# The near tables of a unit written in one transfer and read in one on another queue

## The chip, the cores and the metric

The kernel runs on one core of a Trainium2 chip. The core has TensorE (PE, matmuls), VectorE (DVE), ScalarE (ACT), GpSimd (POOL) and SyncE (SP, which only issues transfers), each with an instruction stream of its own, ordered against the others by semaphores. Transfers run on 16 DMA engines that all issuers share. The metric is the device time of one execution in microseconds.

## The reference

A block of DeBERTa-like attention is followed by a mixture of eight experts, each behind a layernorm. There are 4 x 1024 tokens of 256 channels, in 16 heads of 16. The part that matters here:

```python
scores = jnp.einsum('bhqd,bhkd->bhqk', q, k) / scale
rel = build_relative_position(S, S, BUCKETS, MAX_REL)
c2p_att = jnp.einsum('bhqd,hpd->bhqp', q, pos_k)
c2p = jnp.take_along_axis(c2p_att, clip(rel + ATT_SPAN, 0, 127), axis=-1)
p2c_att = jnp.einsum('bhkd,hpd->bhkp', k, pos_k)
p2c = jnp.swapaxes(jnp.take_along_axis(p2c_att, clip(-rel + ATT_SPAN, 0, 127), axis=-1), -1, -2)
scores = scores + (c2p + p2c) / scale
probs = jax.nn.softmax(scores, axis=-1)
ctx = jnp.einsum('bhqk,bhkd->bhqd', probs, v)
```

The positional terms depend on the distance of query and key alone, and from a distance of 128 on they are constant. So only a band of 384 keys around each block of 128 queries needs a table, the "near" tables; what is constant goes in through extra rows of the matmul ("far").

## The kernel before

The kernel has four stages in a row: `project` (projections of queries, keys and values), `attend` (attention), `mix` (output projection, layernorms, routing) and `experts`. The change touches only `attend`.

`attend` goes over 64 units (4 batches by 16 heads, `N`). A unit has 8 steps (`QT`), one for each block of 128 queries. Each engine runs one loop over s, from -20 (`AHEAD`) to 512 + 13 (`LAG`), and in each pass does some work for several steps at once, at fixed distances:

- `make_table(s + 20)`: PE makes the near values of a block, for both tables (content to position and position to content), and ScalarE's `keep_table` copies them to `table` in SBUF (lines 831 and 832).
- `score(s)`: PE adds the scores of a block; the near part (line 712) needs `near`.
- DVE's `look` and `level` find the row maxima and write the band without them.
- `flip(s - 13)`: PE turns the scores so that keys lie on partitions; ScalarE's `exponent` (line 839) writes the probabilities. `flip` of a step waits for the exponent of the step before it (one for each half).
- `weigh(s - 14)`: PE multiplies by the values (line 749).

Once per unit more is done: `turn_top` on PE at the end of the pass with s % 8 == 1 (line 757), which turns the row maxima for ScalarE's `keep_top` (lines 851 and 853); it waits for the splits that Pool makes of them (lines 926 to 936) and for the table copy of the same pass. The passes of a unit are called steps 0 to 7 here, by s % 8.

**The way of the near tables.** A near table must be skewed: partition p has to see its row shifted by p. The kernel does this through DRAM. `skew_write` stores `table` to `skew_d` with a row pitch of PITCH, and `skew_read` reads it back with a pitch of PITCH - 1. Both are issued by SyncE, and each unit has two halves, `h`. A half of the write is 1 MB in rows of 4 KB (line 629). A read is two transfers (line 639), of 384 KB each for the first half (spots 0 to 2) and of 640 KB each for the second (spots 3 to 7), in pieces of 1 KB. The read waits for the landing of its write (line 636). Then Pool corrects the edges in `near` in five operations for each half (lines 900, 903, 908, 913, 916), in passes that `steps` lists, and reports the half by `near_made`.

SyncE's order in a pass u over units: first half of the write of unit u+2, second half of the read of unit u+1, the four loads of queries and keys of unit u+4 (line 604, which from unit 6 on wait until `flip` is done with unit u-2), every second time three small loads of the far rows (line 615), then the second half of the write and the first half of the read of unit u+2, and the store of the context of unit u-2 (line 645). Each load of line 604 moves 96 KB and comes from a view whose outermost dimension is 3.

ScalarE's queue of its own carries, up to now, the turned maxima (line 853) and 18 small transfers at the start of the stage (line 866), which put constant rows beside the six buffers of queries and keys.

Of the kernel before, what the change touches and what calls it, by code (L numbers as in the profile page):

```python
# [152 lines left out]
def view(t, offset, dims):  # L153

    return bass.AP(tensor=t, offset=offset, ap=dims)
# [362 lines left out]
def attend(nc, sem, spent, masks, rows, split_d, far_d, v_d, skew_d, ctx_d):  # L518
# [14 lines left out]
    PIECES = ((0, 3), (3, QT))  # L533
# [5 lines left out]
    with ExitStack() as ctx:  # L539
# [11 lines left out]
        table = [sb(f"table{i}", [P, 2, 2, 4, SPOT]) for i in range(2)]  # L551
# [17 lines left out]
        rows_set = [sem(f"t_rows_set{i}") for i in range(BUFS)]  # L569
# [4 lines left out]
        skew_out = [[sem(f"t_skew_out{i}{h}") for h in range(2)] for i in range(2)]  # L574
        skew_in = [[sem(f"t_skew_in{i}{h}") for h in range(2)] for i in range(2)]
# [18 lines left out]
        def _(sp):  # L594
# [29 lines left out]
            def skew_write(n, h):  # L624
                sp.wait_ge(table_kept, n * QT + 4 * h + 4)
                if n >= 2:
                    sp.wait_ge(skew_in[n % 2][0], 16 * 2 * (n // 2))
                    sp.wait_ge(skew_in[n % 2][1], 16 * 2 * (n // 2))
                sp.dma_start(view(skew_d, n % 2 * (P * PITCH) + h * 4 * SPOT + 1, [[PITCH, P], [TABLE, 2], [1, 4 * SPOT]]),
                             table[n % 2][:, h, :, :, :].rearrange("p a u v -> p a (u v)")).then_inc(skew_out[n % 2][h], 16)  # L630

            def skew_read(n, h):
                if n >= 2:
                    sp.wait_ge(scored, (n - 2) * QT + 4 * h + 4)
                    sp.wait_ge(seen, (n - 2) * QT + 4 * h + 4)
                sp.wait_ge(skew_out[n % 2][h], 16 * (n // 2 + 1))
                lo, hi = PIECES[h]
                for tab in range(2):
                    sp.dma_start(near[n % 2][:, tab, lo:hi, P:W3],
                                 view(skew_d, n % 2 * (P * PITCH) + tab * TABLE + lo * SPOT + P,  # L640
                                      [[PITCH - 1, P], [SPOT, hi - lo], [1, SPOT]])).then_inc(skew_in[n % 2][h], 16)
# [6 lines left out]
            for u in range(-4, N + 3):  # L648
                if 0 <= u + 2 < N:
                    skew_write(u + 2, 0)  # L650
                if 0 <= u + 1 < N:
                    skew_read(u + 1, 1)
# [11 lines left out]
                if 0 <= u - 2 < N:  # L664
                    store(u - 2)
# [6 lines left out]
        def _(pe):  # L672
# [16 lines left out]
            def score(s):  # L689
# [6 lines left out]
                if t == 0 and n < BUFS:  # L696
                    pe.wait_ge(rows_set[n], 16 * 3)
# [123 lines left out]
        def _(act):  # L821
            def keep_table(x):
                n, u = x // QT, x % QT
                h = u // 4
                act.wait_ge(table_made, x + 1)
                if u % 4 == 0 and n >= 2:
                    act.wait_ge(skew_out[n % 2][h], 16 * (n // 2))
                    act.wait_ge(side_kept, (n - 2) * 2 + h + 1)
                wide = table[n % 2][:, h, :, u % 4, :]
# [16 lines left out]

            def keep_top(n):
# [15 lines left out]
            for i in range(BUFS):  # L863
                for dst, src in ((quest[i][KROWS:FAR, :], ones[0:3, :]), (after[i][FAR:ROWS, :], after_rows[:, :]),
                                 (before[i][FAR:ROWS, :], before_rows[:, :])):
                    nc.scalar.dma_start(dst, src).then_inc(rows_set[i], 16)
            for s in range(-AHEAD, TS + LAG + 1):
# [7 lines left out]
                if s % QT == 4 and 0 <= s // QT + 1 < N:  # L875
                    twin(s // QT + 1)
# [769 lines left out]
```

## Time and profile before

| | |
|---|---|
| median of 3 runs | 1870.73 us (1870.19 to 1876.40) |
| the profiled execution | 1863.67 us, its span 1861.8 us |
| PE busy | 1708.2 us (92%) |
| DVE busy | 1417.6 us (76%) |
| ACT busy | 1163.0 us (62%) |
| POOL busy | 1057.3 us (57%) |
| SyncE's queue in the DMA engines | 393.28 MB, 64.7% of the 16 engines' span |
| ScalarE's queue in the DMA engines | 21.10 MB, 3.6% |
| mean DMA rate | 229 GB/s |

`attend` begins at about 134 us and ends at about 1330 us, and so has two thirds of the span. The page's second part, 40 slices of 46.5 us, shows PE at nine tenths or more from the fifth slice to the 29th with a granted clock of ten tenths. The three slices at the start of the stage and the slices behind it are less full. Durations in the rows are those of instructions; for a transfer the profile has the time of its issue, and as "to landing" the time from the issue to the semaphore. "Idle before, releaser" is what ended an engine's wait. In the waits of SyncE's queue the waiting line is named first, and the operation that released it last.

### The profile page before, as it was taken

What the parts mean: (1) busy time and instruction counts of PE and PEld (TensorE: products, weight loads), DVE (VectorE), ACT (ScalarE), POOL (GpSimd) and SP (SyncE); (2) the same over time, 40 slices, a digit from 0 to 9 for tenths busy, and PEclk for the clock granted to TensorE, in tenths of its full rate; (3) what the DMA queues carried; (4) which work ended last, traced back from release to release, by engine and by line L of the source; (5) the groups of instructions that cost most, each with busy time, mean ns of one, the idle gap of its engine ahead of it and who ended that gap; (6) DMA issues with size and microseconds to landing.
All of it is one profiled execution on the core that took longest, in us unless ns stands there. A gap on an engine that the chain in (4) does not pass through costs nothing. (4 is left out here: it accounts for less than half of the span.)

```text
span 1861.8 us, 41287 instructions
## 1 busy us (share of the span) xinstructions
PE 1708.2 (92%) x13752; PEld 1164.0 (63%) x13752; DVE 1417.6 (76%) x4111; ACT 1163.0 (62%) x2784; POOL 1057.3 (57%) x1260
## 2 busy tenths in 40 slices
PE   7953899999999999999999999999869967999997
PEld 4531565666666666666666666666435656999996
DVE  4751898999999999999999999999534453555553
ACT  6843577788887888888888888787613441222221
POOL 0002777777777777877778777788214321333332
PEclk9985899999999999999999999999955566999998
DMA  5976787878778887788887877877065424666662
GB/s 152 302 259 214 250 277 261 278 256 284 263 257 296 267 276 262 268 285 267 278 276 253 288 260 264 274 262 244 19 169 182 139 74 137 208 189 201 201 198 68
DMA packets 297313, 426.33 MB, mean 229 GB/s; under 512 B 35773, under 2 KB 238545, under 8 KB 297008
## 3 DMA queue, kind: packets, MB, share of 16 engines
q1 hardware_dynamic: 285764, 393.28, 64.7%
q10 hardware_dynamic: 7596, 21.10, 3.6%
q0 software_dynamic: 3744, 9.31, 1.4%
q8 instruction: 112, 1.84, 0.4%
q14 instruction: 97, 0.79, 0.1%
HBM read 245.85 MB, written 178.05 MB: 228 GB/s over the span
## 5 line engine op out<-in xcount | busy, mean ns | idle before, releaser
L839 ACT ACTIVATE t_probsT<-t_flip 128x512 f32<-128x512 f32 x1024 | 626.0, 614 | 201.8 <-PE t_flip L735 148.0
L785 DVE TENSOR_REDUCE t_most<-t_scores 128x1 f32<-128x640 f32 (+1 forms) x512 | 435.0, 850 | 82.1 <-PE t_scores L712 78.8
L804 DVE TENSOR_SCALAR t_band<-t_band,t_top 128x384 f32<-128x384 f32 (+1 forms) x512 | 413.9, 809 | 0.0
L749 PE MATMUL t_sum_ps<-t_probsT,t_vals 128*32 128x256 f32 x4096 | 327.7, 392 | 0.2 <-ACT t_probsT L839 0.2
L831 ACT COPY t_table<-t_table_ps 128x388 f32<-128x388 f32 x512 | 247.9, 484 | 56.3 <-issue 29.0
L916 POOL TENSOR_TENSOR t_near<-t_near,masks 128x768 f32<-128x768 f32 (+1 forms) x128 | 273.5, 2137 | 0.0
L789 DVE CUSTOM_DVE_ANT_0 t_band<-t_scores,t_near 128x384 f32<-128x384 f32 (+1 forms) x512 | 261.6, 511 | 0.0
L735 PE MATMUL t_flip<-masks,t_band 128*128 128x128 f32 x1408 | 261.1, 274 | 0.0
L712 PE MATMUL t_scores<-masks,t_near 128*128 128x128 f32 x1408 | 241.8, 275 | 5.0 <-POOLq L919 5.0
L705 PE MATMUL t_scores<-t_afters,t_quests 105*128 105x256 bf16 (+3 forms) x1024 | 244.0, 288 | 1.3 <-DVE t_most L789 1.3
L900 POOL TENSOR_TENSOR t_near<-t_near,masks 128x384 f32<-128x384 f32 (+1 forms) x128 | 147.1, 1149 | 124.1 <-DMA t_near<-skew_d 117.5
L712 PEld LDWEIGHTS t_scores<-masks,t_near 128*128 128x128 f32 x1408 | 181.7, 143 | 44.5 <-POOLq L919 6.9
L705 PE MATMUL t_scores<-t_befores,t_quests 105*128 105x256 bf16 (+3 forms) x768 | 193.5, 292 | 0.0
L684 PE MATMUL t_table_ps<-rows,t_quests 96*128 96x194 bf16 x512 | 129.7, 253 | 57.5 <-DMA t_quests<-split_d 24.5
L735 PEld LDWEIGHTS t_flip<-masks,t_band 128*128 128x128 f32 x1408 | 163.6, 142 | 0.7
L728 PE MATMUL t_flip<-t_quests,t_befores 108*128 108x512 bf16 (+3 forms) x512 | 161.0, 316 | 0.8 <-ACT t_probsT L839 0.7
L728 PE MATMUL t_flip<-t_quests,t_afters 108*128 108x512 bf16 (+3 forms) x512 | 158.3, 309 | 0.5 <-ACT t_probsT L839 0.2
L1612 PEld LDWEIGHTS e_hid_ps<-e_xT,e_w 128*128 128x128 f32 x1248 | 148.1, 195 | 5.7 <-ACT e_xT L1478 3.7
L1612 PE MATMUL e_hid_ps<-e_xT,e_w 128*128 128x128 f32 x1248 | 148.6, 278 | 3.1 <-ACT e_xT L1478 3.1
L913 POOL TENSOR_TENSOR t_near<-t_near,masks 128x384 f32<-128x384 f32 (+1 forms) x128 | 147.9, 1155 | 0.0
L728 PEld LDWEIGHTS t_flip<-t_quests,t_befores 108*128 108x128 bf16 x512 | 48.9, 96 | 157.0 <-issue 102.3
L832 ACT COPY t_table<-t_table_ps 128x124 f32<-128x124 f32 x512 | 144.3, 282 | 0.0
(194 smaller groups left out, 2670.2 us busy)
## 6 DMA issues: line engine op xcount, KB each, us to landing
skew_d<-t_table SPq DMA_DIRECT2D x128, 1024.0 KB, 9.3
t_near<-skew_d SPq DMA_DIRECT2D x128, 640.0 KB, 8.1
t_near<-skew_d SPq DMA_DIRECT2D x128, 384.0 KB, 7.3
e_w<-in_L_ffn_W_dram ACTq DMA_DIRECT2D x39, 512.0 KB
e_w<-in_L_ffn_W_dram SPq DMA_DIRECT2D x39, 512.0 KB
split_d<-p_part SPq DMA_DIRECT2D x32, 384.0 KB, 3.3
t_afters<-split_d SPq DMA_DIRECT2D x128, 96.0 KB
t_quests<-split_d SPq DMA_DIRECT2D x128, 96.0 KB
```

What stands on the lines that cost most here:

```text
L705: nc.tensor.matmul(out[:, at:at + size], quest[i][0:XROWS, t * P:(t + 1) * P], keys[0:XROWS, piece[0] * P:piece[0] * P + size], start=at % ...
L712: last = nc.tensor.matmul(out[:, (j - lo) * P:(j - lo + 1) * P], near[n % 2][:, 1, j, (t - j + 1) * P:(t - j + 2) * P], ident, start=False ...
L728: last = nc.tensor.matmul(out[:, (a - lo) * P:(z - lo) * P], keys[:, j * P:(j + 1) * P], quest[i][:, a * P:z * P], start=first, stop=False ...
L735: last = nc.tensor.matmul(out[:, (t - lo) * P:(t - lo + 1) * P], band[n % 2][:, t, at:at + P], ident, start=False, stop=True, is_transpose ...
L749: last = nc.tensor.matmul(sum_ps[32 * g:32 * g + 32, 0:2 * P], vals[b % 2][:, j, h * VDIM:h * VDIM + 32], probsT[s % 3][:, g * 2 * P:(g + ...
L785: nc.vector.tensor_reduce(most[:, c, 1:2], out[:, wide:S], AX.X, ALU.max)
L789: nc.vector.tensor_tensor_reduce(band[n % 2][:, t, 0:wide], out[:, 0:wide], near[n % 2][:, 0, t, at:at + wide], 1.0, -3.0e38, ALU.add, ALU ...
L804: nc.vector.tensor_scalar(band[n % 2][:, t, 0:wide], band[n % 2][:, t, 0:wide], top[n % 2][:, t:t + 1], None, ALU.subtract).then_inc(level ...
L831: nc.scalar.copy(ends, table_ps[:, :, 0:FEW].rearrange("p a (e v) -> p a e v", e=2))
L839: nc.scalar.activation(probsT[s % 3][:, half * 512:(half + 1) * 512], flip_ps[half][:, :], ACT.Exp, scale=SCALE).then_inc(expd, 1)
L916: nc.gpsimd.tensor_tensor(tail, tail, masks[:, 1, :].unsqueeze(1).unsqueeze(1).to_broadcast([P, 2, many, P]), ALU.mult).then_inc(edge_made, 1)
L1612: last = nc.tensor.matmul(hid_ps[s % 2][:, c, :], w1[s % WB][:, f, c * P:(c + 1) * P], xT[s % 2][:, f, :], start=(f == 0), stop=(f == 1))
```

## The change

The halves go. `table` gets the layout [P, 2, QT, SPOT], so that a unit's tables lie in one piece of 16 KB per partition. `skew_write(n)` is one transfer of 2 MB by SyncE, issued when all eight blocks of the unit are kept. `skew_read(n)` is one transfer of 2 MB, issued by ScalarE on its own queue in the pass s = 8(n-1), behind the second exponent of that pass; from unit 2 on it waits until unit n-2 is scored and seen, and always for the landing of the write. SyncE's order is now: loads, far loads, write, store. The values of the first batch and the clearing of the old semaphores come later. Pool's steps are set anew: the first half begins two passes later, and its first two operations wait for the whole read. The 18 transfers of constant rows become three, with a source that repeats six times.

The diff, cut to its core:

```diff
-    PIECES = ((0, 3), (3, QT))
-        table = [sb(f"table{i}", [P, 2, 2, 4, SPOT]) for i in range(2)]
+        table = [sb(f"table{i}", [P, 2, QT, SPOT]) for i in range(2)]
-            def skew_write(n, h):
-                sp.wait_ge(table_kept, n * QT + 4 * h + 4)
+            def skew_write(n):
+                sp.wait_ge(table_kept, n * QT + QT)
                 if n >= 2:
-                    sp.wait_ge(skew_in[n % 2][0], 16 * 2 * (n // 2))
-                    sp.wait_ge(skew_in[n % 2][1], 16 * 2 * (n // 2))
-                sp.dma_start(view(skew_d, n % 2 * (P * PITCH) + h * 4 * SPOT + 1, [[PITCH, P], [TABLE, 2], [1, 4 * SPOT]]),
-                             table[n % 2][:, h, :, :, :].rearrange("p a u v -> p a (u v)")).then_inc(skew_out[n % 2][h], 16)
-
-            def skew_read(n, h):
-                if n >= 2:
-                    sp.wait_ge(scored, (n - 2) * QT + 4 * h + 4)
-                    sp.wait_ge(seen, (n - 2) * QT + 4 * h + 4)
-                sp.wait_ge(skew_out[n % 2][h], 16 * (n // 2 + 1))
-                lo, hi = PIECES[h]
-                for tab in range(2):
-                    sp.dma_start(near[n % 2][:, tab, lo:hi, P:W3],
...
+                    sp.wait_ge(skew_in[n % 2], 16 * (n // 2))
+                sp.dma_start(view(skew_d, n % 2 * (P * PITCH) + 1, [[PITCH, P], [1, PITCH]]),
+                             table[n % 2][:, :, :, :].rearrange("p a u v -> p (a u v)")).then_inc(skew_out[n % 2], 16)
...
             for u in range(-4, N + 3):
-                if 0 <= u + 2 < N:
-                    skew_write(u + 2, 0)
-                if 0 <= u + 1 < N:
-                    skew_read(u + 1, 1)
                 if 0 <= u + 4 < N:
                     load_unit(u + 4)
                 if 0 <= u + 2 < N and u % FARS == 0:
                     load_far(u + 2)
-                if u == -4:
+                if 0 <= u + 2 < N:
+                    skew_write(u + 2)
+                if 0 <= u - 2 < N:
+                    store(u - 2)
+                if u == -1:
                     load_vals(0)
+                if u == 1:
                     for semaphore in spent:
                         sp.sem_clear(semaphore)
-                if 0 <= u + 2 < N:
-                    skew_write(u + 2, 1)
-                    skew_read(u + 2, 0)
...
+            def skew_read(n):
+                if n >= 2:
+                    act.wait_ge(scored, (n - 1) * QT)
+                    act.wait_ge(seen, (n - 1) * QT)
+                act.wait_ge(skew_out[n % 2], 16 * (n // 2 + 1))
+                nc.scalar.dma_start(near[n % 2][:, :, :, P:W3].rearrange("p a u v -> p (a u) v"),
+                             view(skew_d, n % 2 * (P * PITCH) + P, [[PITCH - 1, P], [SPOT, 2 * QT], [1, SPOT]])
+                             ).then_inc(skew_in[n % 2], 16)
...
-            for i in range(BUFS):
-                for dst, src in ((quest[i][KROWS:FAR, :], ones[0:3, :]), (after[i][FAR:ROWS, :], after_rows[:, :]),
-                                 (before[i][FAR:ROWS, :], before_rows[:, :])):
-                    nc.scalar.dma_start(dst, src).then_inc(rows_set[i], 16)
+            for dst, src in ((quests[KROWS:FAR, :, :], ones[0:3, :]), (afters[FAR:ROWS, :, :], after_rows[:, :]),
+                             (befores[FAR:ROWS, :, :], before_rows[:, :])):
+                nc.scalar.dma_start(dst, src.unsqueeze(1).to_broadcast([dst.shape[0], BUFS, S])).then_inc(rows_set, 16)
             for s in range(-AHEAD, TS + LAG + 1):
...
                 if s % QT == 4 and 0 <= s // QT + 1 < N:
                     twin(s // QT + 1)
+                if s % QT == 0 and 0 <= s // QT + 1 < N:
+                    skew_read(s // QT + 1)
...
-                    pool.wait_ge(skew_in[i][h], 16 * 2 * (n // 2 + 1))
+                    pool.wait_ge(skew_in[i], 16 * (n // 2 + 1))
...
-            steps = ((8, 1, (3,)), (9, 1, (4,)), (1, 0, (0, 1)), (2, 0, (2,)), (3, 0, (3,)), (4, 0, (4,)),
-                     (5, 1, (0, 1)), (6, 1, (2,)))
+            steps = ((8, 1, (3, 4)), (3, 0, (0, 1)), (4, 0, (2,)), (5, 0, (3,)), (6, 0, (4,)), (7, 1, (0, 1, 2)))
```

## Rows read from the trace of the kernel before

**Rows 1.** Windows: us, busy PE, PEld, DVE, ACT, POOL, clock, DMA share, GB/s

```profile
500.00:700.00 200.00, 198.33 (x1896) 126.41 (x1898) 191.44 (x540) 163.00 (x394) 156.45 (x190) 1.00 0.82 271
```

**Rows 2.** Line 604 alone, 300 to 1300 us: durations, first and last start

```profile
L604 SPq DMA_DIRECT2D t_afters<-split_d x108: 715/730/750, 304.7 to 1250.3; - x108
```

**Rows 3.** Timeline of SyncE: start, us of issue, line, transfer

```profile
643.54 1.51 SPq L604 DMA_DIRECT2D t_afters<-split_d  x2
...
646.60 0.55 SPq L629 DMA_DIRECT2D skew_d<-t_table  x1
...
656.81 1.32 SPq L639 DMA_DIRECT2D t_near<-skew_d  x2
661.35 1.50 SPq L604 DMA_DIRECT2D t_afters<-split_d  x2
...
674.12 0.93 SPq L639 DMA_DIRECT2D t_near<-skew_d  x2
```

**Rows 4.** Waits of SyncE's queue, 300 to 1300 us: total, times, longest

```profile
SPq L636 <- DMA skew_d<-t_table: 197.0, 54, 5.6
```

**Rows 5.** Timeline of ScalarE around its step 0 and step 1

```profile
652.82 0.63 ACT L839 ACTIVATE t_probsT<-t_flip 128x512 f32<-128x512 f32 x1
653.87 0.60 ACT L839 ACTIVATE t_probsT<-t_flip 128x512 f32<-128x512 f32 x1 [0.41 <-PE t_flip L735]
...
654.73 0.28 ACT L832 COPY t_table<-t_table_ps 128x124 f32<-128x124 f32 x1
```

**Rows 6.** Timeline of PE, the turn of the maxima

```profile
655.49 0.22 PE L757 MATMUL t_table_ps<-t_ident,t_top_part 128*24 128x128 bf16 x1
```

**Rows 7.** Windows of 1 us, columns as in rows 1

```profile
655.00:656.00 1.00, 1.00 (x11) 0.35 (x10) 0.97 (x5) 0.73 (x3) 1.00 (x3) 1.00 1.04 404
664.00:665.00 1.00, 1.00 (x14) 0.42 (x13) 0.96 (x6) 1.00 (x4) 0.81 (x1) 1.00 0.20 69
```

**Rows 8.** The write's line alone, 300 to 1300 us

```profile
DMA to landing us min/median/max: 5.4/9.1/12.1
```

**Rows 9.** The issue list of the whole run: KB each, us to landing

```profile
rows<-pick_d SPq DMA_DIRECT2D x1, 1164.0 KB, 9.4
```

**Rows 10.** Timeline of ScalarE at the start of the stage

```profile
152.45 0.74 ACTq L866 DMA_DIRECT2D t_befores<-t_before_rows  x1
153.23 0.49 ACT L831 COPY t_table<-t_table_ps 128x388 f32<-128x388 f32 x1 [29.00 <-issue]
```

**Rows 11.** Windows where PE stood or had stood, columns as in rows 1

```profile
188.00:193.20 5.20, 5.20 (x26) 4.25 (x27) 4.31 (x14) 2.61 (x7) 1.77 (x2) 0.50 0.62 196
...
203.40:210.30 6.90, 6.42 (x31) 4.78 (x32) 5.40 (x15) 3.72 (x9) 3.62 (x3) 0.50 0.70 226
292.80:296.40 3.60, 0.15 (x4) 0.00 (x0) 2.45 (x7) 0.00 (x0) 3.31 (x9) 0.89 0.64 185
296.40:302.40 6.00, 5.94 (x31) 3.65 (x32) 1.79 (x6) 2.80 (x8) 3.68 (x4) 0.50 0.66 220
```

**Rows 12.** Timeline of PE, table matmuls behind a stop

```profile
297.18 0.32 PE L684 MATMUL t_table_ps<-rows,t_quests 96*128 96x194 bf16 x1
...
301.25 0.37 PE L684 MATMUL t_table_ps<-rows,t_quests 96*128 96x194 bf16 x1
```

**Rows 13.** Timeline of POOL: the start of the stage, then one unit

```profile
177.65 1.81 POOL L916 TENSOR_TENSOR t_near<-t_near,masks 128x768 f32<-128x768 f32 x1
...
653.82 0.25 POOL L926 CAST t_top_part<-t_top 128x8 bf16<-128x8 f32 x1 [1.75 <-DVE t_peak L796]
...
659.08 1.00 POOL L900 TENSOR_TENSOR t_near<-t_near,masks 128x384 f32<-128x384 f32 x1 [0.18 <-POOL t_near L916]
...
662.98 1.83 POOL L916 TENSOR_TENSOR t_near<-t_near,masks 128x768 f32<-128x768 f32 x1
665.91 1.29 POOL L900 TENSOR_TENSOR t_near<-t_near,masks 128x512 f32<-128x512 f32 x1 [1.10 <-DMA t_near<-skew_d]
...
668.27 1.04 POOL L908 TENSOR_TENSOR t_near<-t_near,t_side 128x512 f32<-128x512 f32 x1
```

**Rows 14.** Timeline of PE, the first table of the stage

```profile
143.67 0.34 PE L684 MATMUL t_table_ps<-rows,t_quests 96*128 96x194 bf16 x1 [24.50 <-DMA t_quests<-split_d]
```

More of the change, by code:

```diff
@@ L568, in attend @@
         before_set, ident_made, twin_made = sem("t_before_set"), sem("t_ident_made"), sem("t_twin_made")
-        rows_set = [sem(f"t_rows_set{i}") for i in range(BUFS)]
+        rows_set = sem("t_rows_set")
         hats_in = [sem(f"t_hats_in{i}") for i in range(BUFS)]
@@ L573, in attend @@
         vals_in = [sem(f"t_vals_in{i}") for i in range(2)]
-        skew_out = [[sem(f"t_skew_out{i}{h}") for h in range(2)] for i in range(2)]
-        skew_in = [[sem(f"t_skew_in{i}{h}") for h in range(2)] for i in range(2)]
+        skew_out, skew_in = ([sem(f"t_{w}{i}") for i in range(2)] for w in ("skew_out", "skew_in"))
         ctx_out = [sem(f"t_ctx_out{i}") for i in range(2)]
@@ L656, in _ @@
                     load_far(u + 2)
-                if u == -4:
+                if 0 <= u + 2 < N:
[3 more added lines that the diff above has]
+                if u == -1:
                     load_vals(0)
+                if u == 1:
                     for semaphore in spent:
                         sp.sem_clear(semaphore)
-                if 0 <= u + 2 < N:
-                    skew_write(u + 2, 1)
-                    skew_read(u + 2, 0)
-                if 0 <= u - 2 < N:
-                    store(u - 2)
                 if u % BATCH == 4 and u // BATCH + 1 < B:
@@ L695, in score @@
                     pe.wait_ge(ident_made, 1)
-                if t == 0 and n < BUFS:
-                    pe.wait_ge(rows_set[n], 16 * 3)
+                if s == 0:
+                    pe.wait_ge(rows_set, 16 * 3)
                 if t == 0:
@@ L823, in keep_table @@
                 n, u = x // QT, x % QT
-                h = u // 4
                 act.wait_ge(table_made, x + 1)
[L826 to L829, printed above, removed]
+                if u == 0 and n >= 2:
+                    act.wait_ge(skew_out[n % 2], 16 * (n // 2))
+                    act.wait_ge(side_kept, (n - 2) * 2 + 2)
+                wide = table[n % 2][:, :, u, :]
                 ends = view(wide.tensor, wide.offset, [list(wide.ap[0]), list(wide.ap[1]), [SPOT - LEFT, 2], [1, LEFT]])
@@ L887, in keep_side @@
                     pool.wait_ge(edge_made, (n - 3) * 10 + 10)
-                nc.gpsimd.tensor_copy(side[n % 3][:, :, 4 * h:4 * h + 4], table[n % 2][:, h, :, :, BAND]).then_inc(side_kept, 1)
+                nc.gpsimd.tensor_copy(side[n % 3][:, :, 4 * h:4 * h + 4], table[n % 2][:, :, 4 * h:4 * h + 4, BAND]).then_inc(side_kept, 1)
             def edge(n, h, step):
```

2 lines of the change are left out of this document (removed).

## The prediction

> **What bounds the kernel now.** Read first the table by stage. In the attention stage TensorE (PE) is busy 198 of every 200 us at a granted clock of 1.00, while ScalarE has 18.5% of its time free [rows 1]. So nothing that is merely moved can win much there, and whatever makes PE wait lengthens the run. Second, the period: the wait ahead of SyncE's loads passes once per unit (two loads of each kind), and 108 of them lie between 304.7 and 1250.3 us, 53 periods of **17.84 us** [rows 2]; one of eight steps is 2.23 us. Third, SyncE's queue [rows 3], with the reasons for which it stood [rows 4]: for PE ahead of the loads of line 604, for the write's landing ahead of the reads of line 639. Fourth, where ScalarE and PE are within a unit [rows 5, 6]. I set the clock of a unit to zero at its first load, 643.54.
>
> **What is queued where.** The load waits for the flips of step 4 of a unit, so after the change the write of unit n comes out behind the loads of that time, in step 8n-12. The read of unit n is put into ScalarE's program at the end of step 8n-8. In the trace ScalarE ends its last exponent of that step at 653.45, zero plus 9.9 us [rows 5]. From there it is to wait for the landing, with the exponents and the table copies of all later steps behind it.
>
> **When the write has landed.** The write that today follows the same loads is in by the time SyncE issues the read behind it: 656.81 after the loads of 643.54, 674.12 after those of 661.35, that is 13.3 and 12.8 us, mean 13.0 [rows 3]. SyncE really did stand for this landing, 3.6 us each time [rows 4]. Why so long for 1 MB: while only the loads are in flight, the DMA share is 0.20, some 3 of 16 engines at full work, and where a write runs freely it is 1.04 at 404 GB/s [rows 7]. The write is spread over all 16, so its last part waits on the three engines behind the loads. The second megabyte adds 64 KB to each engine, at 404/16 = 25 GB/s 2.6 us. So the 2 MB write lands at 13.0 + 2.6 = **15.6**. The bounds: 13.0, if the second half comes free; and 19.6, if rows of 16 KB go like the nearest long ones (the 12 KB rows of the tables' constants: 1164 KB landed in 9.4 us, where 1 MB of write needs 5.4 at best, so 4.0 more [rows 8, 9]). I take 15.6: the nearest row is the same write with rows of 4 KB.
>
> **What that wait costs.** ScalarE goes on at 15.6, issues the read (0.74 us, its own issues at the start of the stage [rows 10]; bounds 0.4 to 1.3), then an exponent and two copies, 1.15 us from the start of the one (653.87, right behind its first exponent of the step) to the end of the other at 655.01 [rows 5]. PE's turn of the maxima (line 757), at the end of step 1, waits for exactly this copy. It starts today at 655.49, zero plus 11.95 [rows 6]; after the change at 15.6 + 0.74 + 1.15 + 0.1 = 17.6. PE stands **5.65 us** in each unit; 2 us of ScalarE's wait are hidden by the step that PE can still do. Nothing gives this back later, for PE has no idle time to give.
>
> **What the idle time does to the clock.** Three times in this stage PE stood for about 4 us, the last time from 292.8, and each time the granted clock was 0.50 (1.2 instead of 2.4 GHz) when it was busy again, for 5.2, 6.9 and 6.0 us [rows 11]. At that clock a step took 4.07 us (297.18 to 301.25 [rows 12]) against 2.23. So of 6.0 us are lost 6.0 x (1 - 2.23/4.07) = **2.7 us** per unit; nothing, if the clock holds.
>
> **How many units.** Loads that wait go with reads 4 to 61 (loads 6 to 63): **58**. The first units and the last two have no waited load ahead of their write.
>
> **The other parts.** SyncE issues one near transfer per unit instead of six: it is no bound, zero. ScalarE's one issue is in the sum. Pool has the first half two steps later. After the read it needs 5.7 us for half one (659.08 to 664.81), 3.4 for the first three operations of half two (665.91 to 669.31), and 1.7 from the first of the splits (653.82) to the turn (655.49) [rows 6, 13]. The read: today 1.25 MB take 9.10 us from issue (656.81) to Pool's start (665.91) [rows 3, 13]; 0.75 MB more at the 404 GB/s, 2.0 us, so 11.1. From zero to the turn that is 15.6 + 11.1 + 5.7 + 3.4 + 1.7 = 37.5, where 11.95 + 17.84 = 29.8 are there, plus the delay of the unit before (5.65 + 2.7) and the stop itself, 5.65: 43.8. So it lies under ScalarE's wait; with that cover gone it is the third rival.
>
> **Constant rows.** Fifteen of 18 issues of about 0.75 us go. The first copy, today at 153.23 behind the last issue, could follow PE's table of 143.67 [rows 10, 14], some 9 us earlier. But the first near table then needs all eight copies (about 9.4 us, one per 1.25), an 8.0 us write (5.4 alone for 1 MB [rows 8], plus 2.6) and the whole read: 144.3 + 9.4 + 8.0 + 11.1 + 5.7 = 178.5, against 179.46 today [rows 13]. Zero, between -9 and +6.
>
> **Sum.** The profiled execution took 1863.67 us (span 1861.8), 7.1 us or 0.4% under the median of 1870.73; the sum starts there. 58 x (5.65 + 2.7) = 484; 1863.7 + 484 = 2348, rounded **2350 us**.
>
> **Two rules of the Trainium skill.** The page "DMA: Bandwidth & Descriptors" of the Trainium skill, section "Anatomy of one DMA", fits a transfer on GpSimd's path as 2.0 us plus its bytes over 436 GB/s, by estimate 6.8 us for these 2 MB; issued at 3.1 it would land at 9.9, and the run would take some 1925 us by the third rival's path. The loads ahead in the queue are not in that fit. The section "Issuing engines are not separate DMA queues" of that page of the Trainium skill speaks against the change: transfers of different issuers share the same 16 DMA engines, and only issue time is saved. By it the queue of its own gains nothing.
>
> **The rivals.**
> 1. *The same stop, but the clock stays up.* For it: a fall was seen in three places only. Against: this stop is longer than each of the three. 1863.7 + 58 x 5.65 = 2191.
> 2. *The second megabyte comes free.* Landing at 13.0, ScalarE's stop is 3.05 us, 58 x 3.05 = 177: 2041, or with the clock's 2.7 us 2197. Against it: the DMA share is 1.04 already while a write runs.
> 3. *The loads don't hold the write, and Pool becomes the bound.* Issued at 3.1 (646.60 [rows 3]), the write lands 8.0 later as if alone, at 11.1. ScalarE's stop is 1.15 us; the path through read and Pool is 33.0 against 29.8 and passes two stops, so 1.6 each. 58 x 1.6 = 93: 1957. Against: behind these loads today's write needs 10.2 us, almost twice what it needs alone.
> 4. *Long rows are slow*, landing at 19.6: 58 x (9.65 + 2.7) = 716, so 2580.
> 5. *Not slower.* The mechanism: the write moves sooner than today's, because neither a read nor a second write stands beside it on its queue, and has landed before ScalarE asks. It decides at 9.95 us after zero for ScalarE, and at 7.9 for Pool's path (29.8 less 21.9). Then only the start counts, 1855 to 1870. Against it: half the bytes land at 13.0 today. It is also the case in which the change doesn't do what it says, and ScalarE never really waits.
>
> **How the numbers follow.** Forecast 0.50, rival one 0.20, two 0.11, three 0.09, four 0.06, five 0.04, half of it faster by over 0.5% (about what a measurement of this kernel can tell from no change). The forecast's own range is 2230 to 2470 (landing 2 us either way). To hold the time 8 times in 10 the range takes in rivals one and two, and leaves out the others: **2030 to 2520**. Faster 0.02, within 0.5% 0.02, slower 0.96.
>
> **What would show it.** Among the waits of the changed kernel: ScalarE for the DMA of the table write, over 5 us in each of some 58 units, then PE for ScalarE's copy ahead of line 757. A period of 26 us between the waited loads. PE's clock below 1.00 in the whole stage. If it stays 1.00, rival one holds. If PE waits for Pool at the turn and ScalarE for about 1 us, rival three. A write that lands over 15 us after its issue is rival four. The prediction is wrong from the ground up if ScalarE finds the write landed when it comes to the read.

## The result: 2216.7 us where 1870.5 stood, and the profile after

The changed kernel takes 2216.72 us (median of 4 runs, 2212.99 to 2219.08); the kernel before, run beside it, 1870.46 us. The ratio is 1.184, with a 95% interval of 1.181 to 1.187. The forecast was 2350, range 2030 to 2520, slower with a chance of 0.96.

The page of the changed kernel, its first and second parts, then two groups of the fifth (out<-in, count | busy, mean ns | idle before, releaser) and the transfers (KB each, us to landing):

```profile
span 2215.7 us, 40816 instructions
PE 1850.7 (84%) x13752; PEld 1234.9 (56%) x13752; DVE 1416.2 (64%) x4111; ACT 1160.3 (52%) x2784; POOL 1054.8 (48%) x1260
...
PE   8935888788888888888888888878896897699997
...
PEclk9966888888888888888888888888898556799999
...
L820 ACT ACTIVATE t_probsT<-t_flip 128x512 f32<-128x512 f32 x1024 | 624.4, 613 | 571.9 <-DMA skew_d<-t_table 253.6
...
L739 PE MATMUL t_table_ps<-t_ident,t_top_part 128*24 128x128 bf16 x64 | 16.7, 262 | 218.4 <-ACT t_table L813 216.9
...
skew_d<-t_table SPq DMA_DIRECT2D x64, 2048.0 KB, 10.4
t_near<-skew_d ACTq DMA_DIRECT2D x64, 2048.0 KB, 9.0
```

ScalarE, VectorE and Pool do the same work in the same busy time as before. What is new is idle time: ScalarE stands 253.6 us for the landing of the table write, PE 216.9 us for ScalarE. PE is busy 142 us longer with as many matmuls, and the second part says why: its clock reads 8 tenths (80 to 89%) through nearly the whole stage, where it read 9 (90% or more). Line 820 is 839 of before, 739 is 757, 813 is 832, 602 is 604, 626 the write, 833 the read.

The same three questions as in [rows 1, 2, 4]: a stretch of the stage (us, busy PE, PEld, DVE, ACT, POOL, clock, DMA share, GB/s), the load's line alone, and the waits between 400 and 1600 us (total, times, longest):

```profile
500.00:700.00 200.00, 169.55 (x1443) 105.34 (x1435) 144.85 (x408) 121.17 (x294) 117.99 (x147) 0.86 0.60 209
```

```profile
L602 SPq DMA_DIRECT2D t_afters<-split_d x102: 669/692/727, 401.7 to 1596.7; - x102
```

```profile
POOL t_near L891 <- DMA t_near<-skew_d: 454.9, 51, 10.5
...
ACT t_probsT L820 <- DMA skew_d<-t_table: 214.9, 46, 5.7
...
PE t_table_ps L739 <- ACT t_table L813: 185.7, 50, 4.7
```

Over the whole run PE's wait ahead of line 739 has the row (total, times):

```profile
ACT t_table L813: 216.9, 58
```

Every engine does about a quarter less in 200 us. The 102 loads are 51 units, so 50 periods in 1195.0 us: **23.90 us** in place of 17.84. Each unit costs 6.06 us more, and PE stands 58 times; 58 x 6.06 = 351, which added to the 1863.67 of the profiled execution before gives 2215. The profiled execution after took 2217.54. Of its 353.9 us more, 6.6 lie ahead of the first turn of the maxima and 348.2 between the first and the last. The long waits of Pool (10.5 at most) cost nothing: they lie under PE's stop.

One unit of it, on SyncE, ScalarE and PE (start, us, line, operation, idle time before and its end):

```profile
807.13 1.43 SPq L602 DMA_DIRECT2D t_afters<-split_d  x2
...
811.34 0.35 SPq L626 DMA_DIRECT2D skew_d<-t_table  x1
```

```profile
816.42 0.63 ACT L820 ACTIVATE t_probsT<-t_flip 128x512 f32<-128x512 f32 x1
821.85 0.37 ACTq L833 DMA_DIRECT2D t_near<-skew_d  x1
822.32 0.60 ACT L820 ACTIVATE t_probsT<-t_flip 128x512 f32<-128x512 f32 x1 [5.27 <-DMA skew_d<-t_table]
...
823.18 0.28 ACT L813 COPY t_table<-t_table_ps 128x124 f32<-128x124 f32 x1
```

```profile
818.63 0.64 PE L731 MATMUL t_sum_ps<-t_probsT,t_vals 128*32 128x256 f32 x8
823.60 0.27 PE L739 MATMUL t_table_ps<-t_ident,t_top_part 128*24 128x128 bf16 x1 [4.33 <-ACT t_table L813]
...
824.30 0.32 PE L666 MATMUL t_table_ps<-rows,t_quests 96*128 96x194 bf16 x1
...
828.37 0.37 PE L666 MATMUL t_table_ps<-rows,t_quests 96*128 96x194 bf16 x1
...
830.84 0.25 PE L666 MATMUL t_table_ps<-rows,t_quests 96*128 96x194 bf16 x1
```

The write is issued 4.2 us after the load (3.6 in the mean; every second unit has far loads between), ScalarE is done with its exponent at 817.05 and stands until the landing lets it issue the read at 821.85; behind that lie an exponent and two copies, and behind the copies PE's turn of the maxima. Then the table's first matmul, once per step, is 4.07 us from the next one and that 2.47 us from the third. The clock of the same stretches (columns as above):

```profile
819.60:823.40 3.80, 0.00 (x0) 0.00 (x0) 1.59 (x5) 1.08 (x4) 1.47 (x1) 0.82 0.19 39
823.40:828.90 5.50, 5.30 (x28) 3.09 (x29) 1.79 (x6) 2.68 (x8) 0.00 (x0) 0.50 1.05 337
828.90:843.00 14.10, 14.10 (x136) 9.19 (x134) 12.24 (x36) 10.69 (x26) 10.88 (x16) 1.00 0.50 190
```

PE is idle in all of the first, then busy for 5.3 us at 0.50 (1.2 GHz), then at 1.00 until the next stop. Between 400 and 1600 us the clock falls so in each of 50 units. The last part of the write, issued at 811.34 and landed by 821.85, in the same columns:

```profile
811.40:817.00 5.60, 5.60 (x57) 3.35 (x56) 4.70 (x16) 4.60 (x12) 4.32 (x8) 1.00 0.93 370
817.00:821.00 4.00, 2.27 (x25) 1.47 (x21) 3.93 (x12) 0.04 (x1) 3.94 (x5) 1.00 0.28 112
```

After 817 the write is still under way, but the DMA share is 0.28: only a few of the 16 engines are left at work. That fits engines on which the loads stand ahead of the write; experiment e4 comes back to it.

### The profile page after: what moved, and what is told of

Read it like the earlier page. It is cut to its first block and busy times, and to the rows that moved or that the text cites. A ratio compares the mean times of both kernels' runs of the same rounds, so it can differ in the third digit from the quotient of the medians.

```text
span 2215.7 us, 40816 instructions
## 1 busy us (share of the span) xinstructions
PE 1850.7 (84%) x13752; PEld 1234.9 (56%) x13752; DVE 1416.2 (64%) x4111; ACT 1160.3 (52%) x2784; POOL 1054.8 (48%) x1260
## 3 DMA queue, kind: packets, MB, share of 16 engines
q10 hardware_dynamic: 139587, 155.32, 22.8%
## 5 line engine op out<-in xcount | busy, mean ns | idle before, releaser
L820 ACT ACTIVATE t_probsT<-t_flip 128x512 f32<-128x512 f32 x1024 | 624.4, 613 | 571.9 <-DMA skew_d<-t_table 253.6
L731 PE MATMUL t_sum_ps<-t_probsT,t_vals 128*32 128x256 f32 x4096 | 352.9, 419 | 0.2 <-ACT t_probsT L820 0.2
L717 PE MATMUL t_flip<-masks,t_band 128*128 128x128 f32 x1408 | 289.2, 300 | 0.0
L694 PE MATMUL t_scores<-masks,t_near 128*128 128x128 f32 x1408 | 262.6, 294 | 20.4 <-POOLq L910 20.3
L687 PE MATMUL t_scores<-t_afters,t_quests 105*128 105x256 bf16 (+3 forms) x1024 | 260.9, 302 | 3.0 <-DVE t_most L771 2.8
L694 PEld LDWEIGHTS t_scores<-masks,t_near 128*128 128x128 f32 x1408 | 197.7, 153 | 64.3 <-POOLq L910 22.4
L687 PE MATMUL t_scores<-t_befores,t_quests 105*128 105x256 bf16 (+3 forms) x768 | 214.5, 319 | 0.0
L739 PE MATMUL t_table_ps<-t_ident,t_top_part 128*24 128x128 bf16 x64 | 16.7, 262 | 218.4 <-ACT t_table L813 216.9
L710 PE MATMUL t_flip<-t_quests,t_befores 108*128 108x512 bf16 (+3 forms) x512 | 189.3, 371 | 0.7 <-ACT t_probsT L820 0.7
L717 PEld LDWEIGHTS t_flip<-masks,t_band 128*128 128x128 f32 x1408 | 185.6, 159 | 1.9
L666 PE MATMUL t_table_ps<-rows,t_quests 96*128 96x194 bf16 x512 | 140.9, 275 | 40.9 <-DMA t_quests<-split_d 23.2
```

The source lines that it names most:

```text
L687: nc.tensor.matmul(out[:, at:at + size], quest[i][0:XROWS, t * P:(t + 1) * P], keys[0:XROWS, piece[0] * P:piece[0] * P + size], start=at % ...
L694: last = nc.tensor.matmul(out[:, (j - lo) * P:(j - lo + 1) * P], near[n % 2][:, 1, j, (t - j + 1) * P:(t - j + 2) * P], ident, start=False ...
L710: last = nc.tensor.matmul(out[:, (a - lo) * P:(z - lo) * P], keys[:, j * P:(j + 1) * P], quest[i][:, a * P:z * P], start=first, stop=False ...
L717: last = nc.tensor.matmul(out[:, (t - lo) * P:(t - lo + 1) * P], band[n % 2][:, t, at:at + P], ident, start=False, stop=True, is_transpose ...
L731: last = nc.tensor.matmul(sum_ps[32 * g:32 * g + 32, 0:2 * P], vals[b % 2][:, j, h * VDIM:h * VDIM + 32], probsT[s % 3][:, g * 2 * P:(g + ...
L820: nc.scalar.activation(probsT[s % 3][:, half * 512:(half + 1) * 512], flip_ps[half][:, :], ACT.Exp, scale=SCALE).then_inc(expd, 1)
```

## The experiments

My theory was this: a 2 MB write queued behind the loads lands late, ScalarE stands for it, PE behind ScalarE, and each stop costs clock as well. The rivals were that the size of the transfers is the cause, that Pool is, or that the clock only follows and costs nothing.

**The write ahead of the loads** (e1). This is the changed kernel with SyncE's order turned round:

```diff
+                if 0 <= u + 2 < N:
+                    skew_write(u + 2)
                 if 0 <= u + 4 < N:
                     load_unit(u + 4)
                 if 0 <= u + 2 < N and u % FARS == 0:
                     load_far(u + 2)
-                if 0 <= u + 2 < N:
-                    skew_write(u + 2)
```

> The changed kernel with one edit: in SyncE's order the write of a unit's tables comes ahead of the loads of that pass. Theory one (the loads in front hold the write, and ScalarE waits for it): the write is issued about 2 us before zero (zero: the first waited load) instead of 3.1 to 4.2 us behind it, lands about 8 us later, near 6, and ScalarE finds it landed when it asks at 9.9. ScalarE's wait and PE's stop go, the clock stays at 1.00, the period falls from 23.9 to about 17.9, the run to 1860 to 1900; Pool's path from ScalarE's issue to the turn of the maxima (0.4 + 9.2 + 5.7 + 3.4 + 1.7 = 20.4 behind 9.9, so 30.3) is then just at the 29.8 us that are there. Theory two (merging the halves itself is what costs, as 16 KB rows or as a read that Pool gets whole and late): the period stays at 20 us or more, the run above 2000 us. The output is complete.

It takes 1909.19 us, ratio 1.0205 (1.0188 to 1.0222). From a ratio of 1.1841 to 1.0205 is 306 of the 344 us by which the ratio says the change is slower, for one order of issues. The time lies above the 1900 at most of the first theory, and far below the 2000 of the second. ScalarE's wait for the write is gone from the list of waits, and the write lands 7.7 us after its issue at the median, where it was 10.5. What is left, 38 us, goes with three units that take 11 to 13 us longer than the others, 37 in all. One of them, on SyncE, ScalarE, Pool and PE:

```profile
577.20 0.43 SPq L619 DMA_DIRECT2D t_vals<-v_d  x1
```

```profile
580.31 0.37 ACTq L833 DMA_DIRECT2D t_near<-skew_d  x1
```

```profile
600.13 0.99 POOL L891 TENSOR_TENSOR t_near<-t_near,masks 128x384 f32<-128x384 f32 x1 [13.49 <-DMA t_near<-skew_d]
```

```profile
600.92 0.40 PE L710 MATMUL t_flip<-t_quests,t_afters 108*128 108x256 bf16 x1 [9.34 <-DMA t_quests<-t_topT]
```

The values of a batch (1152 KB) leave on SyncE's queue 3.1 us before the read leaves on ScalarE's. The read is in after 19.8 us instead of 9.2, and the turned maxima (6 KB), issued behind it on ScalarE's queue at 584.02, are late too. It is for these, and not for Pool, that PE stands. From 595 to 600.9 us the DMA share is only 0.19, so few engines hold up what is left; which transfers keep those busy I haven't traced.

**The read on SyncE** (e2). This is the changed kernel, loads still first, but the read waits and is issued on SyncE behind the store, so ScalarE never stands for the write:

```diff
                     store(u - 2)
+                if 0 <= u + 2 < N:
+                    skew_read(u + 2)
...
-                if s % QT == 0 and 0 <= s // QT + 1 < N:
-                    skew_read(s // QT + 1)
```

> The changed kernel with the whole read issued by SyncE, behind the store of the same pass, instead of by ScalarE. SyncE can stand for the landing without holding anybody's exponents. Theory one (ScalarE's standing is what stops PE now, Pool's path lies under it): ScalarE's wait for the write is gone, but PE now stops for Pool ahead of the turn: landing 14.6 + read 9.3 + Pool's 10.8 = 34.7 against 29.8, shared by two stops, about 2.5 us per unit; the run at 2000 to 2030 if the clock holds, up to 2130 if it falls behind each stop. Rival (Pool's late start is already the bound of the changed kernel): no gain, 2190 to 2230. Rival two (the wait on ScalarE is all there is): 1870 to 1900.

It takes 2014.40 us, ratio 1.0766 (1.0745 to 1.0788). From the waits between 400 and 1200 us:

```profile
POOL t_near L891 <- DMA t_near<-skew_d: 239.6, 39, 9.1
...
PEld t_table_ps L750 <- POOL t_top_part L927: 43.0, 33, 2.4
PE t_scores L705 <- POOLq L910: 42.0, 22, 3.2
```

Now PE waits for Pool: for the split maxima and for the near tables. That is rival three's path, laid bare with ScalarE's wait gone. It costs 20.44 - 17.84 = 2.6 us per unit, part of which is the clock (it falls in 17 of the 39 units, for 3.4 us each). So the write behind the loads is dear on either engine's way, and the other 3.5 us come only with ScalarE's wait.

**Extra matmuls in the gap** (e3). This is the changed kernel, with 16 matmuls in fp32 (32 records) ahead of PE's wait for the turn:

```diff
             def turn_top(n):
+                for _ in range(FILL):
+                    nc.tensor.matmul(sum_ps[:, 2 * P:3 * P], ident, ident, start=True, stop=True, skip_group_check=True)
                 pe.wait_ge(split_made, 5 * (n + 1))
```

> The changed kernel with 16 matmuls more in each unit, ahead of the wait of the turn of the maxima, into a part of a PSUM bank that nobody reads; they add work where PE stands idle for about 4 us. Theory (part of the loss is the clock that falls behind each idle stop): the granted clock stays at or near 1.00 in the attention stage, each unit becomes about 2 us shorter though PE does more, 2090 to 2110 us. Rival (the clock has nothing to do with the idle time, or costs nothing because PE is not the bound behind the stop): 2217 us or more, up to 230 us more if the added matmuls stand on the path. The output is complete.

The added matmuls write columns that nothing reads, but they start sums of their own in the bank in which the weighted values are being summed. So, other than the expectation has it, this kernel's weighted sums are changed, and its output with them; its time is read for the clock alone. Behind the last turn of the maxima it takes 534 us, the changed kernel 533, so the wrong values do not change the time of the later stages.

It takes 2117.56 us, ratio 1.1318 (1.1295 to 1.1341): with more work per unit it is 98 us faster by the ratios, though 8 us above the 2110 that I expected at most. The same 200 us, first of the changed kernel and then of this one, and its filler:

```profile
300.00:500.00 200.00, 169.51 (x1428) 104.89 (x1426) 144.76 (x403) 121.53 (x296) 114.81 (x142) 0.86 0.57 198
```

```profile
300.00:500.00 200.00, 196.90 (x1833) 135.68 (x1833) 145.19 (x434) 131.82 (x320) 124.88 (x153) 1.00 0.63 220
```

```profile
800.27 3.84 PE L739 MATMUL t_sum_ps<-masks 128*128 128x128 f32 x32
```

The clock stays at 1.00, the period falls from 23.89 to 21.89 us, and ScalarE and Pool, whose work is unchanged, do 8% and 9% more in the stretch. At least 2.0 of the 6.06 us per unit were thus the clock and not the wait.

**Loads spread over the engines** (e4). This is the changed kernel, with each of the four loads of a unit cut from an outermost dimension of 3 into three transfers of 16 partitions:

```diff
-    HATS = 4
+    HATS = 12
...
+                    for w in range(PARTS):
+                        sp.dma_start(dst[w * DH:(w + 1) * DH, :], view(split_d, at + w * step, [[S, DH], [1, S]])
+                                     ).then_inc(hats_in[i], 16)
```

> The changed kernel with the four loads of a unit cut into twelve of 16 partitions each, so that each spreads over 16 DMA engines instead of 3; the bytes and the place ahead of the write are the same. Theory (the three engines that carry the loads hold the last part of the write): the data of the loads takes about 1 us of all engines instead of 6 to 8 us of three; SyncE needs longer to issue twelve (0.4 to 0.7 us each, 5 to 8 us, which pushes the write's issue from 3.1 to 5 to 8), so the landing comes at 13 to 16 and the time is between 2080 and 2240, with the write 8 to 9 us from issue to landing instead of 10.4. Rival (the write is slow by itself, through its 16 KB rows): issue to landing stays above 10 us.

It takes 2145.22 us, ratio 1.1466 (1.1443 to 1.1488). Its issues of one unit, on SyncE and ScalarE:

```profile
818.30 2.63 SPq L603 DMA_DIRECT2D t_afters<-split_d  x6
820.98 2.73 SPq L603 DMA_DIRECT2D t_quests<-split_d  x6
...
824.82 0.34 SPq L628 DMA_DIRECT2D skew_d<-t_table  x1
```

```profile
833.36 0.37 ACTq L835 DMA_DIRECT2D t_near<-skew_d  x1
```

Between the issue of the write and that of the read lie 7.2 us in the mean, where it was 10.5. But twelve issues take SyncE 3.0 us longer, and the write leaves at zero + 6.6 instead of 3.6. From zero to the read it is 13.8 against 14.1. So the landing comes only 0.3 us sooner. A rival has to be met: a write that leaves 3 us later finds less of the loads' data ahead of it, however these are spread. How the write ends speaks for the engines (columns as above):

```profile
829.00:831.00 2.00, 1.44 (x15) 0.69 (x13) 1.97 (x6) 0.00 (x0) 1.84 (x5) 1.00 0.80 319
831.00:833.30 2.30, 0.00 (x0) 0.00 (x0) 2.27 (x7) 0.00 (x0) 2.30 (x2) 1.00 0.06 15
```

Here the DMA share is still 0.80 up to 6.2 us behind the issue, and then nearly all data are in. In the changed kernel it was down to 0.28 from 5.7 us on. So the few engines of the loads did hold the write's last part; how much of the 3.3 us is theirs and how much the later issue's is not shown. The period is 22.8 us, 1.1 less; the other 0.8 is not traced.

**The second-half read alone on ScalarE** (e9). This is the kernel before, its halves and all else kept, with only this moved:

```diff
-                if 0 <= u + 1 < N:
-                    skew_read(u + 1, 1)
...
+                if s % QT == 0 and 0 <= s // QT + 1 < N:
+                    skew_read_late(s // QT + 1, 1)
```

> The kernel before with one part of the change alone: the read of the second half is issued by ScalarE, at the place where the change puts its read (end of step 0 of the unit before), still two transfers of 640 KB behind a write of 1 MB, which SyncE issues behind the loads as ever. Theory (ScalarE's wait for a write that stands behind the loads is the whole price, whatever the size): in the kernel before this write lands 13.0 us after zero, ScalarE asks at 9.9, and PE stops for 13.0 + 0.7 (two issues) + 1.15 + 0.1 - 11.95 = 3.0 us in each of 58 units, which is 1870 + 174 = 2045; with a clock that falls behind some of the stops (up to 2 us each) up to 2160. Rival (the megabyte-size transfers of the change are what costs, the queue does not matter): 1865 to 1880.

It takes 2047.41 us, ratio 1.0948 (1.0905 to 1.0990). Its wait between 400 and 1300 us:

```profile
PE t_table_ps L755 <- ACT t_table L830: 85.0, 43, 2.8
```

It is the same mechanism with writes of 1 MB: 2.0 us of stop in each of 43 units where I had expected 3.0, and a period of 20.7 us. Between 400 and 1300 us, the stretch with these 43 stops, the granted clock falls 20 times, 17 times for 3.4 us and three times for twice as long. One of the stops and the clock behind it, on PE and as a window:

```profile
442.05 0.22 PE L755 MATMUL t_table_ps<-t_ident,t_top_part 128*24 128x128 bf16 x1 [1.92 <-ACT t_table L830]
```

```profile
442.30:445.70 3.40, 3.40 (x18) 2.25 (x21) 0.24 (x1) 1.89 (x6) 3.34 (x4) 0.50 1.00 328
```

So the joined halves and the 16 KB rows are not needed for the loss. The wait on ScalarE, for a write behind loads, brings about half of it by itself (177 of 346 us); the second megabyte makes the wait longer.

**The remaining 39 us, and a version that keeps the idea** (e5). The write goes first, and the values of a batch go in eight parts in eight passes. Beside the order of e1 the edit is:

```diff
-                if u % BATCH == 4 and u // BATCH + 1 < B:
-                    load_vals(u // BATCH + 1)
+                if 4 <= u % BATCH < 4 + QT and 0 <= u and u // BATCH + 1 < B:
+                    load_vals(u // BATCH + 1, [u % BATCH - 4])
```

> The first experiment's kernel (write ahead of the loads), and the values of a batch are loaded in eight transfers of 144 KB in eight successive passes instead of one of 1152 KB. In the first experiment three places, each behind a load of values, cost some 13 us each, and the period between them was near 17.9. Theory one (in the changed kernel only the order on SyncE's queue cost time, the merged transfers by themselves cost nothing once the write is issued ahead of the loads; what is left are three collisions of the values with the read): 1909 less 39, so 1865 to 1880, no difference from the kernel before that can be measured. Rival (the whole read, which Pool gets late, leaves no margin, so that the remaining 2% stay): 1895 to 1910.

It takes 1871.57 us, ratio 1.0031 (1.0016 to 1.0045). The three stops are gone: from 220 us to the end of the stage the clock doesn't fall. What is left is at the start. Pool's first operation on a near table there, in this kernel:

```profile
188.44 0.99 POOL L892 TENSOR_TENSOR t_near<-t_near,masks 128x384 f32<-128x384 f32 x1 [28.43 <-DMA t_near<-skew_d]
```

**The same with the read on SyncE** (e8). It is e5 with the edit of e2:

> As the first of these runs (write ahead of the loads, values in parts), but the read is issued by SyncE behind the store instead of by ScalarE. What the queue of ScalarE gives by itself: with the write landed before ScalarE asks, nobody waits for it there. On SyncE the read stands behind the loads in program order, whose wait passes at zero, some 10 us ahead of the earliest time of the read in the same unit, and behind the store. Theory (the 16 DMA engines are shared, the queue gives nothing): within 0.5% of the first of these runs. Rival (a read on the queue of its own starts earlier or flows better): slower than that run by 1% or more, by a later start of Pool in every unit.

It takes 1861.07 us (1858.65 to 1862.72), ratio 0.9973 (0.9960 to 0.9985): the fastest kernel of this study, ahead of both. Run on the same chip as e5, it is 10.5 us under it, and the start accounts for it:

```profile
173.76 0.99 POOL L892 TENSOR_TENSOR t_near<-t_near,masks 128x384 f32<-128x384 f32 x1 [15.81 <-DMA t_near<-skew_d]
```

That is 14.7 us sooner than in e5. The first turn of the maxima comes 12.9 us sooner (201.5 against 214.4), and the two profiled executions are 12.9 us apart (1860.74 and 1873.63). The steady periods are 17.84 and 17.90 us. So the queue of its own brings nothing in the steady part, and costs at the start. Both expectations missed this: the one said within 0.5%, and it is 0.6% by the ratios; the other said slower. One thing beside the queue differs there: SyncE, which now has to issue the reads in its turn, lets the values go at 179.05, where in e5 they leave from 168.98 on.

**The values whole again, on one queue** (e10). It is e8 with the values in one transfer:

> As the eighth run (write ahead of the loads, read issued by SyncE), but with the values of a batch in one transfer of 1152 KB again. In the first experiment (read on ScalarE's queue) each of the three loads of values held a read up, by about 13 us. Theory (two queues share the 16 DMA engines, so that a load on the one slows a read on the other, while on one queue the read, issued when its turn comes, stands ahead of or right behind the values): at most half of these 39 us come back, 1861 to 1880. Rival (the size of the load of values alone does it, whatever the queue): 1895 to 1905.

It takes 1868.17 us, ratio 0.9988 (0.9978 to 0.9998). By the ratios the same 1152 KB cost 1.7%, 33 us, beside a read on a second queue (e1 less e5), and 0.15%, 3 us, on one queue (e10 less e8; those intervals overlap). From 200 us on the longest landing of a read is 12.7 us here and 19.8 in e1. But two things besides the queue are other than in e1, and I did not separate them: SyncE's order puts the read ahead of the values (561.79 and 562.23, where in e1 the values leave 3.1 us earlier than the read), and the turned maxima, for which PE stood in e1, have ScalarE's queue to themselves.

**Values in parts, on the kernel before** (e7). It has such a stop too, at 292.8 [rows 11]; the edit is that of e5 for the values:

> The kernel before, only the values of a batch are loaded in eight parts over eight passes. In its trace the single stop of the attention stage that is longer than 1 us (292.8 to 296.4, followed by 6.0 us at half clock) lies behind the load of values of 1152 KB. Theory (that load delays a near read): the stop and its clock loss go, 1870 less 7, so 1861 to 1866, and the trace keeps the clock at 1.00 from 220 to 1340 us. Rival (the stop comes from the filling of the pipeline): 1870.

It takes 1874.39 us, ratio 1.0034 (1.0012 to 1.0055). Half of this theory fell. The stop did go:

```profile
292.80:296.40 3.60, 3.60 (x39) 2.51 (x41) 3.57 (x9) 2.98 (x8) 2.34 (x1) 1.00 0.79 306
```

But the time did not fall with it: over the whole stage the period is 18.11 us instead of 17.81, and between 400 and 1200 us Pool waits 169 us for the reads instead of 69. I have not shown which transfers the parts delay.

**The constant rows alone** (e6). It is e7 with the three transfers of constant rows:

> The kernel before with the change's three transfers of constant rows instead of 18, and with the values of a batch in eight parts over eight passes. Against the next run, which has the parts of the values alone, it gives the price of the constant rows. The prediction's step says zero, between -9 and +6 us. Here the halves are kept, so that the first near table could come up to 9 us earlier: -3 to -9 us against the next run, 1855 to 1862. Rival (the way of the first near tables hangs on something else, so that the free issue time of ScalarE is idle time): within 2 us of the next run.

It takes 1869.68 us, ratio 1.0004 (0.9982 to 1.0026); against e7, on the same chip, 4.7 us less, though the intervals overlap: the twelve times go from 1858.57 to 1875.31 here and from 1857.06 to 1877.36 there. The start is clearer: Pool's first operation begins at 169.58 us instead of 174.95, and the first turn of the maxima 5.3 us sooner. So this part of the change gains some 5 us at the start. That they reach the whole time is not shown, and the 1855 to 1862 that I expected did not come; of the two profiled executions that of e6 is the longer, by 2.1 us.

## Why the prediction was right, and where its sizes were off

**The mechanism and its place** were as predicted: ScalarE stands for the write, PE for ScalarE's copy ahead of the turn, in 58 units (216.9 us, 3.7 each), the clock at 0.50 behind each stop. The three terms of the steady part (landing, issue and clock) were all too large; 58 x (5.65 + 2.7 - 6.06) = 133 is what 2350 was too high by.

**Landing.** Predicted 15.6 after zero, measured 14.1 (13.4 to 15.1 in 51 units, from the load's start to the read's issue). Two parts of it: I took 13.0 for the first megabyte from two rows, and over all units of before that mean is 12.4; and I took 2.6 for the second, where it came to 1.7. A free write shows the same: 2 MB land in 7.2 us at the least (e1, from 200 us on), 1 MB in 5.4 [rows 8], so 1.8 for the second. The step that was mis-sized is thus the price of a further megabyte as a plain rate. At 1.7 us it would be some 600 GB/s, more than the 471 at most that the write of 811.34 shows in any window of 1 us, so the difference is no rate at all. In the kernel before, a read of 768 KB and the next write stand behind the first megabyte [rows 3]; whether they slow it is not traced. The read, too, was set too long: 11.1 us predicted, 9.0 measured (the median to landing).

**The issue on ScalarE.** Predicted 0.74 from the small transfers of constant rows, measured 0.37.

**PE's stop.** 5.65 predicted. Taking off 1.5 and 0.37 leaves 3.8, and the waits say 185.7 / 50 = 3.7. So the working behind the landing (exponent, two copies, turn) was right.

**The clock.** Predicted 2.7 per unit, from 6.0 us at half speed. The period's excess less the stop is 6.06 - 3.7 = 2.35, and 5.3 busy us at 0.50 with the step ratio of [rows 12] make 5.3 x (1 - 2.23/4.07) = 2.4. Experiment e3 gives back 2.0 of it. The argument against rival one, that this stop is longer than the three of before, does not hold: it came to 3.7 us, and those were 3.5 to 3.8. The clock fell all the same, and in e9 behind a stop of 1.9. The sum from measured terms is 58 x (3.7 + 2.35) = 351.

**The start.** Predicted zero, between -9 and +6. Measured +10 at Pool's first operation (183.99 against 174.04) and +6.6 at the first turn of the maxima (209.9 against 203.3). The rows in three transfers by themselves gain 5 us (e6). What I missed is what stands beside the read on the other queue: I timed the first read as if alone (11.1 us), and it shares the engines with what stands on SyncE's queue. ScalarE issues it at 161.04; the queues between 166 and 183 us (packets, MB, share of 16 engines):

```profile
q1 hardware_dynamic: 1256, 3.41, 54.9%
q10 hardware_dynamic: 2654, 2.70, 52.0%
```

Half of the engines' time goes to SyncE's queue (q1: the write of unit 1, the values, the loads, all issued after the read), and Pool has the read 23 us after its issue. In e8 the same read, issued at 160.00 on the one queue ahead of the write and the loads, with the values held back as said, is there after 13.8.

**The rules.** The Trainium skill's page "DMA: Bandwidth & Descriptors", section "Issuing engines are not separate DMA queues", says that issuing from several engines saves no more than issue time; e5 against e8 agrees, and shows a loss of 10.5 us. The same page of the Trainium skill, section "Queues, rings and completion order", says that each DMA engine takes packets in turn from the queues that have work; the 54.9% and 52.0% above agree. The fit in its section "Anatomy of one DMA", which the Trainium skill gives for GpSimd's path, makes 6.8 us for 2 MB by estimate. The rows have 7.2 us at the least and 7.7 at the median where the write goes first (e1), so for a free transfer the fit would have been 0.4 to 0.9 us short; behind the loads it took 10.5.

**The rivals.** Rival one's number, 2191, lies nearer to 2217 than my own, but its mechanism is false: the clock fell in every unit. Its number came near by luck: it took a stop 1.95 us too long and left out a clock loss of 2.35. Rival two with the clock's loss has the nearest number of all, 2197, by luck as well: the second megabyte wasn't free (1.7 us), its landing at 13.0 was 1.1 too early, and its clock loss of 2.7 made up for part of that. Rival three is out as it stands, since the loads do hold the write; its path through read and Pool lay hidden and came out in e2 once ScalarE was free. Rival four is out, since the write with 16 KB rows took 10.5 us against 9.1 for half the bytes [rows 8]. Rival five's case did not come, but the point at which it decides was right: e1 brings the landing ahead of ScalarE's arrival, and ScalarE stands no more.

## What to carry to other kernels

Before a wait for a transfer is put on an engine, look at what stands in that engine's program behind the wait and what stands ahead of the transfer on its queue: here one order of issues on SyncE was worth 306 of 344 us. A transfer that someone will soon wait for is issued ahead of loads that have units of time to spare. Put on the same queue as these, with them behind it, it cost less here than on a queue of its own (e8 against e5). And a stop of PE of some 4 us in every unit costs more than its length, here 6.06 us for 3.7. The joined transfers are not what cost the time: with the order mended, and the values in parts, they run within 0.3% of the kernel before (e5, e8).

## What the runs showed of the hardware that I had not expected

- **Idle time that costs less when filled.** Sixteen useless fp32 matmuls per unit made the changed kernel 98 us faster (ratio 1.132 against 1.184), since the clock stayed at 1.00.
- **Bulk on a second queue goes with a late urgent transfer.** A 2 MB read took 9.2 us at the median, and 19.8 us when 1152 KB stood on the other queue (e1); on one queue, ahead of them, the longest was 12.7 (e10, both from 200 us on). At the start it was 23 against 13.8 to Pool's operation. How much of it is the queue and how much the order is not separated.
- **Loads with an outermost dimension of 3 hold back what comes behind them.** From the issue of the write to that of the read it is 10.5 us behind them, and 7.2 when they are cut to 16 partitions each, with the same bytes and the write issued 3.0 us later; the share of 0.28 at the write's end becomes 0.80.
- **A large issue is not a dear one.** The 2 MB read costs its issuer 0.37 us, the turned maxima 0.76 us (824.19, line 843), and a load with an outermost dimension of 3 about 0.7 us (669 to 727 ns). But the time isn't fixed: at the start of e8 the write at 162.69, 2.7 us behind a 2 MB read on its queue, takes 5.37 us to issue, where its median is 0.32.
- **A stop of 1.9 us can bring the clock down.** In e9 the granted clock fell 20 times in a stretch with 43 stops of 2.0 us in the mean and 2.8 at most; behind one of 1.92 us it was 0.50 for 3.4 us.
